# Linear-attention and expert block on 8 cores: layer-norm statistics in batches of four groups, and the output stage after LN2

## What is computed

```python
xn = layernorm(x)                                  # no gamma, no beta
# linear attention on xn, then a post-norm block
Q = elu(xn@Wq+bq)+1;  K = elu(xn@Wk+bk)+1;  V = xn@Wv+bv
KV = einsum('nshd,nshm->nhmd', K, V);  Ksum = K.sum(axis=1)
Z = 1 / (einsum('nlhd,nhd->nlh', Q, Ksum) + 1e-6)
a = layer_norm(xn + einsum('nlhd,nhmd,nlh->nlhm', Q, KV, Z)@Wo + bo, g1, beta1)
attn = layer_norm(a + relu(a@W1+b1)@W2 + b2, g2, beta2)
# 8 experts; a row's two experts follow from a hash of its first two columns
for e in range(8):
    out += w_e * (relu(xn@W1e+b1e)@W2e + b2e)      # w_e is 0.5 or 0 for each row
result = x + attn + out
```

## Time and profile before

| | us |
|---|---|
| timed runs (2) | 5849.72 and 6291.06, median 6070.39 |
| profiled execution, own time | 5847.35 |
| span of its slowest core | 5845.8 |
| span of its fastest core | 5834.9 |
| mean granted TensorE clock, each core | 0.908 to 0.909 |

### The profile page before, as it was taken

The page is one execution under the profiler, slowest core; times in us unless marked ns, Lnnn a source line. Parts: engine busy times, 40 slices in busy tenths (PEclk is TensorE's granted clock), DMA queues, the critical chain, the costliest instruction groups (busy, mean ns, idle before and its releaser), DMA issues.

```text
span 5845.8 us, 55993 instructions; the slowest of 8 cores (5834.9 to 5845.8 us)
## 1 busy us (share of the span) xinstructions
PE 4863.0 (83%) x21665; PEld 2130.7 (36%) x21665; DVE 1698.3 (29%) x3206; ACT 1139.1 (19%) x2204; POOL 344.3 (6%) x660
## 2 busy tenths in 40 slices
PE   4777499999999999999999999999986443777742
PEld 2333144444444444444444444444432110333311
DVE  2444222222222222222322222222224224111144
ACT  3444111111111111111111111111102113111111
POOL 1000000000000000000000000000000000000000
PEclk8778799999999999999999999999988665999965
DMA  3000022222222222222222222222212110111112
GB/s 59 30 32 27 14 40 39 35 38 38 37 37 38 37 37 38 37 37 39 38 35 38 38 35 38 38 35 39 40 22 35 43 38 6 27 25 26 27 38 83
DMA packets 105684, 209.48 MB, mean 36 GB/s; under 512 B 12960, under 2 KB 13232, under 8 KB 105424
## 3 DMA queue, kind: packets, MB, share of 16 engines
q0 software_dynamic: 91056, 163.84, 18.4%
q1 hardware_dynamic: 14368, 42.06, 2.2%
HBM read 361.06 MB, written 8.39 MB: 63 GB/s over the span
## 4 chain that ended last, share of the span: by engine, by line
PE 78%; DVE 8%; ACT 6%; issue 3%; DMA 3%; POOL 0%; DVEq 0%; ACTq 0%; SPq 0%; POOLq 0%
PE ps L726 31%; PE ps L764 31%; PE ps L1113 4%; PE ps L1092 4%; PE ps L475 3%; DMA xt_b<-xs 1%; ACT h_b L1102 1%; PE ps L770 1%; PE ps L455 1%; DVE x_sb L1130 1%; DMA xtm_b<-xs 1%; DVE ln_t L1050 1%; PE ps L953 1%; DVE acc L788 1%; DVE scol L414 1%
## 5 line engine op out<-in xcount | busy, mean ns | idle before, releaser
L726 PE MATMUL ps<-xnbf,w1s 128*128 128x512 bf16 x8192 | 1828.5, 382 | 53.7 <-DVE wb L711 32.4
L726 PEld LDWEIGHTS ps<-xnbf,w1s 128*128 128x128 bf16 x8192 | 800.0, 98 | 1048.8 <-issue 109.6
L764 PE MATMUL ps<-h_hi,w2s 128*128 128x512 bf16 x4096 | 923.6, 384 | 22.5 <-DVE acc L788 22.5
L764 PE MATMUL ps<-h_lo,w2s 128*128 128x512 bf16 x4096 | 904.9, 379 | 0.0
L788 DVE TENSOR_TENSOR acc<-acc,ps 128x512 f32<-128x512 f32 x992 | 614.9, 681 | 836.5 <-PE ps L764 534.0
L736 ACT ACTIVATE h_lo<-ps,eb_sb 128x512 bf16<-128x512 f32 x512 | 309.8, 688 | 1545.2 <-PE ps L726 1545.2
L764 PEld LDWEIGHTS ps<-h_hi,w2s 128*128 128x128 bf16 x4096 | 404.5, 99 | 522.0 <-issue 51.5
L736 ACT ACTIVATE h_hi<-ps,eb_sb 128x512 bf16<-128x512 f32 x512 | 309.8, 688 | 1461.7 <-PE ps L726 1461.7
L764 PEld LDWEIGHTS ps<-h_lo,w2s 128*128 128x128 bf16 x4096 | 400.7, 98 | 483.3
L744 DVE TENSOR_TENSOR h_lo<-h_lo,wb 128x512 bf16<-128x512 bf16 x512 | 183.2, 419 | 951.4 <-ACT h_lo L736 951.4
L744 DVE TENSOR_TENSOR h_hi<-h_hi,wb 128x512 bf16<-128x512 bf16 x512 | 183.1, 419 | 898.1 <-ACT h_hi L736 898.1
(11 more groups left out here) (178 smaller groups left out, 2280.9 us busy)
## 6 DMA issues: line engine op xcount, KB each, us to landing
w1s<-ew_pk POOLq DMA_DIRECT2D x256, 256.0 KB, 3.6
w2s<-ew_pk POOLq DMA_DIRECT2D x256, 256.0 KB, 3.5
xtm_a<-xs SPq DMA_DIRECT2D x32, 512.0 KB, 3.3
xt_b<-xs SPq DMA_DIRECT2D x32, 256.0 KB, 2.6
w1s<-w_pk POOLq DMA_DIRECT2D x32, 256.0 KB, 3.6
w2s<-w_pk POOLq DMA_DIRECT2D x32, 256.0 KB, 3.6
xtm_b<-xs SPq DMA_DIRECT2D x16, 512.0 KB, 4.1
out<-otm_b SPq DMA_DIRECT2D x16, 512.0 KB, 2.9
```

Source lines behind the costliest of these rows:

```text
L726: self.em("T", lambda t, k=k, tt=tt, slot=slot: t.matmul(ps[tt][:], self.w1t(slot, k), self.xnbf[:, k * TOWN + tt * 512:k * TOWN + (tt + 1 ...
L764: self.em("T", lambda t, j=j, tt=tt, slot=slot, hreg=hreg, lp=last_plain: t.matmul(ps[4 + tt][:], self.w2t(slot, j), hreg[:, j * TOWN + tt ...
```

## The change

Phase A takes its statistics in batches of four groups. `stats_sums(g)` loads and forms the sums of one group and subtracts the mean; `stats_finish(gs)` forms 1/sqrt for four groups at once on four columns and scales the four groups' rows. `xtm_a` has four slots, the squares have their own buffer `sq2`. Within a batch, each group is transposed and projected, then the sums of the group four later are emitted, then the group's ELU (`elu_all`, not threaded any more) and its KV products. After four groups comes `stats_finish` for the next four. The Newton step moves from ScalarE to VectorE. For own groups one copy of the mean (VectorE) and one of 1/sqrt (ScalarE) are added.

LN2 loses its hook. LN2 runs through all quarters, a barrier follows, then B4 with its 16 groups, with its buffers in the region of LN2's temporaries and PSUM banks 0 to 3.

```diff
-        self.s_lx = [mk("lx0"), mk("lx1")]
+        self.s_lx = [mk("lx0"), mk("lx1"), mk("lx2"), mk("lx3")]
+        self.sq2 = sb("sq2", [128, 2 * D], F32, 49664, 65536)
-        self.xtm_a = sb("xtm_a", [128, 2 * D], F32, TR, 196608)
+        self.xtm_a = sb("xtm_a", [128, 4 * D], F32, TR, 196608)
...
-        self.xtm_b4 = sb("xtm_b4", [128, 2 * D], F32, XB, 163840)
-        self.otm_b4 = sb("otm_b4", [128, 2 * D], F32, XB + 8192, 163840)
+        self.xtm_b4 = sb("xtm_b4", [128, 2 * D], F32, TR, 196608)
+        self.otm_b4 = sb("otm_b4", [128, 2 * D], F32, TR + 8192, 196608)
...
-        def emit_stats(g, mid_v=None, mid_s=None):
+        def stats_sums(g):
...
+            if g >= 4:
+                self.wait("Y", self.s_mm, evT[g - 4])
+            evDMA[g] = self.dma("Y", xt, self.xs[g * 128:(g + 1) * 128, :], self.s_lx[g % 4])
...
+            self.wait("V", self.s_lx[g % 4], evDMA[g])
             if g >= 2:
+                self.wait("V", self.s_ve, evSQ.get(g - 2, 0))
+            self.em("V", lambda v: v.reduce_sum(mc, xt, axis=AXX))
+            self.vbar()
+            self.em("V", lambda v: v.tensor_scalar_mul(mc, mc, -INV_D))
             v_negm = self.inc("V", self.s_ve, 1)
             self.wait("S", self.s_ve, v_negm)
...
+            self.em("S", lambda s: s.activation(sq, xt, AF.Square, bias=mc))
+            self.chain("S", self.s_sc)
+            self.em("S", lambda s: s.add(xt, xt, mc))
+            s_sub = self.inc("S", self.s_sc, 1)
+            self.wait("V", self.s_sc, s_sub)
+            self.em("V", lambda v: v.reduce_sum(ac, sq, axis=AXX))
+            evSQ[g] = self.inc("V", self.s_ve, 1)
+            self.wait("V", self.s_ve, evSQ[g])
+            if own:
+                mm_dst = self.mstat[:, g:g + 1]
+                self.em("V", lambda v: v.tensor_copy(mm_dst, mc))
+                self.vbar()
+
+        def stats_finish(gs):
...
+            self.em("V", lambda v: v.tensor_scalar(a, a, INV_D, EPS_LN, op0=OP.mult, op1=OP.add))
+            v_ac = self.inc("V", self.s_ve, 1)
+            self.wait("S", self.s_ve, v_ac)
+            self.em("S", lambda s: s.activation(r0, a, AF.Ln))
+            self.chain("S", self.s_sc)
+            self.em("S", lambda s: s.activation(r0, r0, AF.Exp, scale=-0.5))
+            s_r0 = self.inc("S", self.s_sc, 1)
+            self.wait("V", self.s_sc, s_r0)
+            self.em("V", lambda v: v.tensor_mul(rcb, r0, r0))
+            self.vbar()
+            self.em("V", lambda v: v.tensor_mul(rcb, rcb, a))
+            self.vbar()
+            self.em("V", lambda v: v.tensor_scalar(rcb, rcb, -0.5, 1.5, op0=OP.mult, op1=OP.add))
+            self.vbar()
+            self.em("V", lambda v: v.tensor_mul(rcb, rcb, r0))
+            v_rcb = self.inc("V", self.s_ve, 1)
+            self.wait("S", self.s_ve, v_rcb)
+            for j, g in enumerate(gs):
...
+                self.em("S", lambda s, xt=xt, rc=rc: s.mul(xt, xt, rc))
+                self.chain("S", self.s_sc)
+                if own:
+                    self.em("S", lambda s, rr=self.rstat[:, g:g + 1], rc=rc: s.copy(rr, rc))
+                    self.chain("S", self.s_sc)
+                    self.em("S", lambda s, xt=xt, g=g: s.copy(self.xn01[:, g:g + 1], xt[:, 0:1]))
+                    self.chain("S", self.s_sc)
+                    self.em("S", lambda s, xt=xt, g=g: s.copy(
+                        self.xn01[:, NGOWN + g:NGOWN + g + 1], xt[:, 1:2]))
+                    self.chain("S", self.s_sc)
+                evA[g] = self.s_sc.n
...
-        pend = []
-        for g in range(NGL):
-            if pend:
-                pg, ek, ev = pend.pop(0)
-                emit_stats(g, mid_v=lambda pg=pg, ek=ek: elu_vmax(pg, ek),
-                           mid_s=lambda pg=pg, ek=ek, ev=ev: (elu_sexp(pg, ek),
-                                                             elu_vtail(pg, ev)))
-                emit_kv(pg)
-            else:
-                emit_stats(g)
-            ek, ev = emit_T(g)
-            pend.append((g, ek, ev))
...
+        nbat = NGL // 4
+        for g in range(4):
+            stats_sums(g)
+        stats_finish([0, 1, 2, 3])
+        for b in range(nbat):
+            gs = [4 * b + j for j in range(4)]
+            nxt = [4 * (b + 1) + j for j in range(4)] if b + 1 < nbat else []
+            for j, g in enumerate(gs):
+                emit_trans(g)
+                emit_proj(g)
+                if nxt:
+                    stats_sums(nxt[j])
+                elu_all(g)
+                emit_kv(g)
+            if nxt:
+                stats_finish(nxt)
...
-            if tt_hook is not None:
-                tt_hook(tt, max(evApply[(tt, c)] for c in range(KC)))
...
-    def emit_b4_group(self, j, evAdd):
+    def emit_b4(self):
...
-                self.emit_ln(2, tt_hook=b4hook)
-                self.emit_b4(skip=NGOWN)
...
+            self.emit_ln(2)
+            self.barrier()
+            self._dump("accf", self.acc)
+        if "B4" in phases:
             self.emit_b4()
```

More of the change, by code:

```diff
@@ L405, in emit_stats @@
             if g >= 2:
-                self.wait("S", self.s_mm, evKVmm.get(g - 2, 0))
[L407 to L414, removed]
@@ L415, in emit_stats @@
-            self.vbar()
[L416 to L424, removed]
@@ L435, in emit_stats @@
[L435 to L449, removed]
+                self.wait("S", self.s_ve, evSQ.get(g - 2, 0))
@@ new lines, in elu_all @@
+        def elu_all(g):
+            rt = self.elu_a[:, (g % 2) * D:(g % 2 + 1) * D]
+            kslot = self.ktm[:, (g % 2) * D:(g % 2 + 1) * D]
+            vslot = self.vtm[:, (g % 2) * D:(g % 2 + 1) * D]
+            self.wait("V", self.s_mm, evKmm[g])
+            if g >= 2:
+                self.wait("V", self.s_mm, evKVmm.get(g - 2, 0))
+            for hh in range(2):
+                self.em("V", lambda v, hh=hh: v.tensor_scalar(
+                    rt[:, hh * 512:(hh + 1) * 512], ps[hh][:], 0.0, None, op0=OP.max))
+            evK_v[g] = self.inc("V", self.s_ve, 1)
+            self.wait("S", self.s_mm, evKmm[g])
+            self.wait("S", self.s_ve, evK_v[g])
+            if g >= 2:
+                self.wait("S", self.s_mm, evKVmm.get(g - 2, 0))
+            for hh in range(2):
+                self.em("S", lambda s, hh=hh: s.activation(
+                    kslot[:, hh * 512:(hh + 1) * 512], ps[hh][:], AF.Exp))
+            evK_s[g] = self.inc("S", self.s_sc, 1)
+            self.wait("V", self.s_sc, evK_s[g])
+            for hh in range(2):
+                self.em("V", lambda v, hh=hh: v.scalar_tensor_tensor(
+                    kslot[:, hh * 512:(hh + 1) * 512], kslot[:, hh * 512:(hh + 1) * 512],
+                    1.0, rt[:, hh * 512:(hh + 1) * 512], op0=OP.min, op1=OP.add))
+            self.vbar()
+            self.wait("V", self.s_mm, evVmm[g])
+            for hh in range(2):
+                self.em("V", lambda v, hh=hh: v.tensor_copy(
+                    vslot[:, hh * 512:(hh + 1) * 512], ps[2 + hh][:]))
+            evV_v[g] = self.inc("V", self.s_ve, 1)
@@ L461, in emit_T @@
                 self.wait("S", self.s_mm, mmv)
-                if (not own) and g >= 2:
+                if (g >= NGOWN) and g >= 2:
                     self.wait("S", self.s_mm, evKVmm.get(g - 2, 0))
@@ L494, in emit_T @@
                     start=False, stop=True))
-            evVmm = self.inc("T", self.s_mm, 1)
-            return evKmm, evVmm
-        def elu_vmax(g, evKmm):
-            par = g % 2
-            rt = self.elu_a[:, par * D:(par + 1) * D]
-            self.wait("V", self.s_mm, evKmm)
-            if g >= 2:
-                self.wait("V", self.s_mm, evKVmm.get(g - 2, 0))
-            for hh in range(2):
-                self.em("V", lambda v, hh=hh, rt=rt: v.tensor_scalar(
-                    rt[:, hh * 512:(hh + 1) * 512], ps[hh][:], 0.0, None, op0=OP.max))
-            evK_v[g] = self.inc("V", self.s_ve, 1)
@@ L509, in elu_sexp @@
-        def elu_sexp(g, evKmm):
-            par = g % 2
-            kslot = self.ktm[:, par * D:(par + 1) * D]
-            self.wait("S", self.s_mm, evKmm)
-            self.wait("S", self.s_ve, evK_v[g])
-            if g >= 2:
-                self.wait("S", self.s_mm, evKVmm.get(g - 2, 0))
-            for hh in range(2):
-                self.em("S", lambda s, hh=hh, kslot=kslot: s.activation(
-                    kslot[:, hh * 512:(hh + 1) * 512], ps[hh][:], AF.Exp))
-            evK_s[g] = self.inc("S", self.s_sc, 1)
@@ L521, in elu_vtail @@
[L521 to L536 removed]
+            evVmm[g] = self.inc("T", self.s_mm, 1)
@@ L969, in emit_b1, with emit_ln @@
                 evX1par[n % 2] = self.inc("V", self.s_ve, 1)
-    def emit_ln(self, which, tt_hook=None):
+    def emit_ln(self, which):
         ps = self.ps
```

166 lines of the change are left out of this document (65 added, 101 removed).

## The result

| | before | after |
|---|---|---|
| median of the timed runs | 5870.18 us (10 runs) | 5979.74 us (11 runs) |
| lowest run | 5846.53 | 5974.22 |
| profiled execution, own time | 5847.35 | 5974.22 |
| span of its slowest core | 5845.8 (core 0) | 5972.6 (core 7) |

The ratio is 1.0199, with a 95% interval from 1.0165 to 1.0233. Of the seven runs of before in the ratio five lie at 5846.53 to 5849.72 and two higher, at 5890.63 and 5911.27; their mean is 5863.1, that of the nine of after 5979.9. The kernel is slower by 2.0%; whether by more than 2% the interval leaves open. Lowest against lowest the ratio is 1.0218.

The account below looks back on a forecast made before the run. It took the chain of hand-overs between engines, none of them full, as the bound. Terms 31+8+63+21.5+10 = 134 us on the profiled 5847.35 gave 5981 us, 2.3% more, range 5945 to 6020.

Parts of the forecast that it names:

- the exposed wait in B4: VectorE's wait for each B4 load, put at 5.09 us in 15 intervals; 4.58 for a load on time.
- K's end: In a phase A turn, the K projection was to end 9.9 us in, leaving VectorE 1.9 us late.
- Part 1, the sums on the path: Phase A turns: next batch's load and sums delay ELU, KV products and next transposes; +31 us, plus 8 for late loads.
- The tail: Phase A loads that land later than the median: 0.3 us per load, 28 loads, +8 us.
- the rival of sums that fit under K: Phase A: load and sums finish before the K projection does; total 78 us, time 5925; chance 0.10.
- Part 2, the batch end: Every fourth phase A group: chain and four multiplications precede evacuation; extra 7.6 us, own 11.0, seven ends, +63 us.
- Part 3, the start: Phase A's start: three more groups' sums and four multiplications before the first evacuation, loads hidden under weight loading; +21.5 us.
- The last batch: Phase A's last four groups: no sums to compute, -0.27 us each, -1 us.
- sign of phase A over near 715 to 720: Expected in the profile after: phase A over near 715 to 720 us instead of 597 to 604.
- Part 4, LN2 then B4: The end: LN2 148.8 us, then B4 with 15 exposed loads; 252.7 against 242.3 us, +10.
- The rival on the clock: Phase A: TensorE stays at half clock, 28 groups x 4.7 = 132 us more, time 6113; chance 0.05.
- a bound of +22: Phase A's KV products at half clock, twice 0.8 us: +22 us on the range's high end.

Follow-up runs that it names:

- late_load: Kernel after, with the load of group i+4 issued only when group i's K projection is done: 6205.07 and 6205.79 us.
- slots8: Kernel after, with eight slots for x instead of four, so each load is issued a batch earlier: 5917.91 to 5921.73 us, ratio 1.0131.
- early_finish: Kernel after with eight slots, multiplications spread behind evacuations, next batch's 1/sqrt ahead of the last group's ELU: mostly 5843.73 to 5852.36 us, ratio 0.9999.
- lead: `early_finish` with the transposes of group g+1 put ahead of the KV products of group g: 5772.91 to 5777.19 us.

## Why the prediction came out as it did

The predicted time was 5981, the measured median 5979.74, inside the range of 5945 to 6020. The direction and the place were right: phase A carries the loss, LN2 with B4 next to nothing. That the totals lie 1.3 us apart is luck: the profiled execution took 5974.22, 7 us less than the forecast, and the terms missed in both directions.

**The step that failed** is the last one, from the sum to the claim. I set 134 us on a base of 5847.35, called it 2.3%, and gave 0.70 to slower by over 2%; the ratio is 1.0199, and its interval holds 2%. The growth came nearly as forecast, 129 us by the mean of the cores. But the seven runs of before in the ratio average 5863.1, 16 us above my base, and I had put such scatter at nothing, with 17 us between the forecast and the threshold. The claim was neither confirmed nor refuted, and did not deserve so much of the chance. Inside the sum the mis-sized terms are the exposed wait in B4 (5.09 us, measured 4.73), K's end (9.9, measured 11.3) and the start, whose loads were to cost nothing under the weight loading and cost 2 to 3 us.

**The base.** The sum stands on the profiled 5847.35 and not on the 6070.39 that was then the median of two runs. Ten runs put the median of before at 5870.18 and its lowest at 5846.53. Against 6070.39 the same 5981 would be a gain of 1.5%, which no stage of the trace shows.

**Part 1, the sums on the path.** The chain was right link by link: load, two sums, ELU, KV products. Other groups took 18.65 us a turn, predicted 18.35 + 0.3. Own groups took 19.2, 0.3 more than their 18.6 + 0.3, or some 5 us over 16. The tail is confirmed by itself: from the issue of a load to the row sum behind it core 7 takes 3.6 us on average over the 28, which is the 3.3 + 0.3 of the sum. One step was wrong in detail, K's end at 9.9. I read it in a turn of before and kept it, though I had myself noted that TensorE would idle longer ahead of it. It is 11.3, so VectorE is 1.0 late. The sum did not depend on it, since it followed VectorE; but the rival of sums that fit under K was nearer than I wrote, 1.0 us away and not 1.9. And 41 of the 45 us by which `late_load` missed are this step.

**Part 2, the batch end.** Over two turns at a batch end the extra on core 7 was 10.3 us where own groups are prepared (49.3, 49.0 and 47.9, on average 48.7, less 2 x 19.2) and 7.6 otherwise (44.8, 45.3 and 44.8, less 2 x 18.65): predicted 11.0 and 7.6, in sum 61.3 against 63. I had looked for one turn of 26 to 30. The extra is split over two turns of 21 to 25 instead, since the first transposes are early and only their evacuation is late.

**Part 3, the start.** The first evacuation starts at 75.94, predicted about 73, before 51.59: +24.3 rather than +21.5. I had the loads of all four groups land under the weight loading, and so cost nothing. They do land there, but they cost. VectorE begins once the last of the weights and constants has landed, and that comes later the more loads were issued ahead of it. Its first instruction in before (core 0, two loads ahead), in after (core 7, four) and in `slots8` (core 3, eight):

```profile
38.22 0.91 DVE L371 MEMSET m_sb<- 128x1024 bf16 x1 [38.22 <-DMA nwc_sb<-nwc_c]
```

```profile
40.33 0.91 DVE L372 MEMSET m_sb<- 128x1024 bf16 x1 [40.33 <-DMA nwc_sb<-nwc_c]
```

```profile
47.28 0.91 DVE L372 MEMSET m_sb<- 128x1024 bf16 x1 [47.28 <-DMA nwc_sb<-nwc_c]
```

`nwc_sb` is issued at 19.3 in all three and lands 18.5, 20.6 and 27.6 us later. Of the 24.3 us, 2.1 are this. From the first row sum to the first multiplication it is 26.2 us instead of 9.4, 16.8 more (predicted 17.0 - 0.8), and from there to the evacuation 8.4, predicted 8.3.

**The last batch.** It has no sums to form. I gave it -1 and it gave about -4: one turn there is 14.2 us, since K took 3.61 us at full clock (TensorE, core 7).

```profile
702.39 0.63 PE L505 MATMUL ps<-ident,xtm_a 128*128 128x128 f32 x4
...
705.99 3.61 PE L527 MATMUL ps<-wk_sb,xnp 128*128 128x512 bf16 x16 [1.28 <-ACT xnp L516]
...
716.60 0.63 PE L505 MATMUL ps<-ident,xtm_a 128*128 128x128 f32 x4
```

With these, phase A is 24.3 + 12 x 1.63 + 16 x 1.59 + 61.3 - 4 = 126.6, of 129.7 measured; the rest is what single turns differ from these means. All of it lies ahead of the last group: the first transposes of group 31 stand at 716.60 and in before at 586.78, 129.8 apart. My sign of phase A over near 715 to 720 was a slip against my own +124: the last addition (L575) is at 735.0, before 605.0.

**Part 4, LN2 then B4.** LN2 took 148.2, predicted 148.8. B4 took 98.0 and not 103.9: the mis-sized term is its interval, 5.09 + 1.28 = 6.37, where 6.02 was measured. The waits of VectorE on core 7, from the last barrier on, with its first two additions from the timeline:

```profile
DVE otm_b L1162 <- DMA xtm_b<-xs: 74.3, 16, 5.9
```

```profile
5878.04 1.28 DVE L1162 TENSOR_TENSOR otm_b<-xtm_b,ps 128x512 f32<-128x512 f32 x2 [3.35 <-DMA xtm_b<-xs]
5883.88 1.29 DVE L1162 TENSOR_TENSOR otm_b<-xtm_b,ps 128x512 f32<-128x512 f32 x2 [4.55 <-DMA xtm_b<-xs]
```

The 15 waits behind the first take (74.3 - 3.35)/15 = 4.73 each, nearer to the 4.58 that I gave as the lower bound. I had taken the 5.09 from core 0 of before, with its late load of 7.0 in 12 waits; core 3 of before has 57.2 us in 12, 4.77. 15 x 0.36 = 5.4 us too much.

**What no term held.** The untouched stages differ by 7 us between the two slowest cores, and my +134 met a span that grew by 127. On core 3 the growth is 137, by the mean of all eight 129.1. Against the table phase A was 6 too low, LN2/B4 and the choice of core 13 too high; against the mean phase A was 3.6 too low and LN2/B4 4.2 too high, and the untouched stages, which I had at 0, gave 3.8 back. Either way errors cancel in the total.

**The rival on the clock** had 0.05 as a clock that stays at half for a whole turn, which did not happen: the V products take 3.63 us in every turn shown. A smaller form of it did. The KV products ran at half clock in 13 of 31 groups of core 7, 0.4 us each, some 5 us in sum: I had that as a bound of +22, for all turns, and as a sign of being wrong. In `slots8` (core 3) it happens in none of 31. From 100 to 580 us core 0 of before runs at a mean clock of 0.79; core 7 of after, from 100 to 650 us, at 0.74; `early_finish` is at 0.83:

```profile
100.00:580.00 480.00, 354.42 (x1741) 153.02 (x1739) 225.36 (x386) 177.46 (x425) 0.00 (x0) 0.83 0.07 25
```

For the whole phase I can't split the 59 us of `slots8` into wait and clock, only for the two turns compared above: the earlier load changes both.

## What to carry to other kernels

When work is put into an engine's in-order list, its price is what now stands behind it, and a load that it waits for has to land by the time the list reaches it: four more slots were worth 59 us here, while the turns of `early_finish`, 0.7 us shorter than those before the change, only paid for its later start. The kernel before was beaten only where work was put into a wait, in `lead` and in the loads of B4. Loads issued early are not free either when something else must land first: two more at the start cost 2 us, six more 9. When work for several groups is batched, put between the batch and the first consumer only what that consumer needs; the rest, four multiplications here, goes behind the evacuation. Read a wait that becomes a term of the sum from several cores, and give little chance to a claim whose forecast lies a third of a per cent from its threshold.

## What the hardware showed that I had not expected

**The clock fell after short pauses too.** In `lead` the recorded pauses of TensorE in the turn from 503.98 are 1.06 us between the two waves of transposes and 0.66 ahead of K at 507.61. The granted clock is full up to the start of K all the same and falls to 0.50, 1.2 GHz, in its first products at 508. In the turn from 90.5, with pauses as short (1.01 and 0.63), it stays at 1.00, 2.4 GHz. What tells these turns apart, the traces do not show me. A turn costs 11.7 us in the one case and 13.5 to 16 in the other.

The Trainium skill (TensorE: Matmul & The Clock Gate, A second HAM failure mode: psum-queue depth-cycling) describes, beside the case of long waits for data, a kernel in which TensorE idles only briefly but often between groups of matmuls and the clock swings all the same. The trace of `lead` agrees with that; no run here shows what would stop it.

**Two loads of 512 KB and a store under way at once on every core**: a load takes 5.3 us by the median, against 4.0 where one load follows each store, and 3.3 in phase A, where a core has one load under way. In phase A most of them, not all: the view of `xtm_a` of after has 3.1/3.3/12.3 us for shortest, median and longest. The 12.3 is the last of the four issued together at the start, beside the weights; the median of those four is 7.9.
